# An edge mask and edge counts built in DRAM tables by indirect DMAs, in place of one-hot matrix products

## What is computed

```python
def _build_mask(edge_index, edge_type, edge_type_weights, dtype):
    src, dst = (edge_index[0], edge_index[1])
    w = jax.nn.softplus(edge_type_weights)
    mask = jnp.full((N, N), -jnp.inf, dtype=dtype)
    mask = mask.at[src, dst].set(w[edge_type - 1])        # the last edge wins
    diag = jnp.diagonal(mask)
    mask = mask.at[idx, idx].set(jnp.where(jnp.isneginf(diag), w[3], diag))
...
scores = jnp.einsum('hnd,hmd->hnm', q2, k2) * scale + mask[None]   # layer 0, 16 heads
...
deg = jax.ops.segment_sum(jnp.ones_like(col), col, num_segments=n) # layer 1, 4 hops
dis = jnp.clip(deg, 1.0) ** (-0.5)
norm = dis[row] * dis[col]
msg = norm[:, None] * alpha * x_j                                  # one per edge
agg = jax.ops.segment_sum(msg, col, num_segments=n)
```

## Time and profile before

| | us |
|---|---|
| median of 3 runs | 799.48 (799.28 to 799.86) |
| the profiled execution, its own time | 800.38 |
| its span in the profile | 798.6 |
| PE busy in the span | 775.6 (97%) |
| DVE busy | 583.9 (73%) |
| ACT busy | 387.0 (48%) |
| POOL busy | 48.2 (6%) |

### The profile page before, as it was taken

The page is one execution under the profiler, slowest core; times in us unless marked ns, Lnnn a source line. Parts: engine busy times, 40 slices in busy tenths (PEclk is TensorE's granted clock), DMA queues, the critical chain, the costliest instruction groups (busy, mean ns, idle before and its releaser), DMA issues. The chain is left out here.

```text
span 798.6 us, 11507 instructions
## 1 busy us (share of the span) xinstructions
PE 775.6 (97%) x4270; PEld 685.8 (86%) x4270; DVE 583.9 (73%) x1234; ACT 387.0 (48%) x800; POOL 48.2 (6%) x88
## 2 busy tenths in 40 slices
PE   5999999999999999999998899999999999999998
PEld 5888878889999999998875488888888879999886
DVE  7988888646644798997688968889886676674341
ACT  5222113344533676765767646574683342454220
POOL 3000000000000000001102211000002020000000
PEclk9999999999999999999999999999999999999999
DMA  5522114433334333319975349224134245334331
GB/s 190 185 81 78 56 56 138 137 118 106 106 125 129 103 100 97 95 55 319 269 244 129 132 121 261 96 89 158 53 124 128 72 113 138 133 133 158 126 125 39
DMA packets 28775, 102.17 MB, mean 128 GB/s; under 512 B 3736, under 2 KB 3864, under 8 KB 28464
## 3 DMA queue, kind: packets, MB, share of 16 engines
q1 hardware_dynamic: 24784, 86.76, 32.3%
q0 software_dynamic: 3936, 14.68, 8.4%
HBM read 91.99 MB, written 1.57 MB: 117 GB/s over the span
## 5 line engine op out<-in xcount | busy, mean ns | idle before, releaser
L1200 DVE TENSOR_TENSOR w_lo<-raw,w_hi 128x1024 fp32r<-128x1024 f32 x140 | 169.9, 1222 | 65.1 <-ACT w_hi L910 64.7
L910 ACT ACTIVATE w_hi<-raw 128x1024 fp32r<-128x1024 f32 x140 | 147.3, 1057 | 105.7 <-PE bank L1984 79.6
L1932 PE MATMUL bank<-xn1T,w_hi 128*128 128x384 f32 x416 | 106.8, 337 | 0.0
L1984 PE MATMUL bank<-w_hi,xn3T 128*128 128x512 f32 x288 | 92.0, 393 | 0.0
L1932 PEld LDWEIGHTS bank<-xn1T,w_hi 128*128 128x128 f32 x416 | 74.2, 188 | 0.9 <-issue 0.3
L1932 PE MATMUL bank<-xn1T,w_lo 128*128 128x384 f32 x208 | 69.6, 335 | 0.0
L1984 PEld LDWEIGHTS bank<-w_hi,xn3T 128*128 128x128 f32 x288 | 54.1, 188 | 11.0
L1932 PE MATMUL bank<-xn4T,w_hi 128*128 128x384 f32 x240 | 61.1, 335 | 0.0
L1984 PE MATMUL bank<-w_lo,xn3T 128*128 128x512 f32 x144 | 56.0, 389 | 0.0
L1932 PEld LDWEIGHTS bank<-xn4T,w_hi 128*128 128x128 f32 x240 | 43.2, 188 | 0.0
L1932 PE MATMUL bank<-xn4T,w_lo 128*128 128x384 f32 x120 | 40.1, 335 | 0.0
(11 more groups left out here) (363 smaller groups left out, 1712.0 us busy)
## 6 DMA issues: line engine op xcount, KB each, us to landing
raw<-weights SPq DMA_DIRECT2D x140, 512.0 KB, 3.3
row_sb<-rows SPq DMA_DIRECT2D x6, 512.0 KB, 5.6
kcat<-kcat POOLq DMA_DIRECT2D x16, 192.0 KB, 2.9
base<-rows POOLq DMA_DIRECT2D x6, 512.0 KB, 13.8
w2r<-w_in SPq DMA_DIRECT2D x1, 2048.0 KB, 10.5
w1r<-w_in POOLq DMA_DIRECT2D x1, 2048.0 KB, 9.7
x_sb<-x_in SPq DMA_DIRECT2D x3, 512.0 KB, 4.9
row_sb<-rows SPq DMA_DIRECT2D x6, 256.0 KB, 4.8
```

The source lines that it names most:

```text
L910: act.activation(w_hi[:, u % RING], raw[:, u % RAW], ACT.Copy).then_inc(hi_split, 1)
L1200: dve.tensor_tensor(w_lo[:, u % RING], raw[:, u % RAW], f(w_hi[:, u % RING]), ALU.subtract).then_inc(unit_split, 1)
L1932: last = pe.matmul(out_of(pr)[:, 0:N], w[pa][:, slot, k * P:(k + 1) * P], TT[src][:, pb, k], start=(k == 0 and m == 0), stop=(k == KD - 1 ...
L1984: last = pe.matmul(out_of(pr)[:], tile[:, pa, k, ts], w[pb][:, at_, j * HALF:(j + 1) * HALF], start=(kk == 0 and j == 0 and m == 0 and nam ...
```

## The change

The mask and the counts are built in two tables in DRAM, each of 384x384 numbers and 512 spare cells. POOL fills them with zeros or with the value for no edge, by two plain DMAs, and then writes the edges by indirect DMAs, one for each chunk of 128 edges and table, four chunks to a step: 48 that write the value of the edge's type to the mask table, 48 that add to the count table, and three that write the diagonal first. Since one edge may hit the cell of another, each step of 512 edges is freed of duplicates before: DVE now compares each chunk with all four chunks of its group (L1331 after the change, 128x512), with a triangular matrix `later` that gives 4096 for a later edge and 1 otherwise. The sum of a row is 4096 or more where a later edge of the step has the same cell, and such an edge is sent to a spare cell; else it is the number of edges of the step in that cell, which is what is added to the count. A step's four writes to a table wait until the four of the step before have landed. At the end POOL loads both tables back into SBUF. The one-hot products and matrices, and the steps graph, counts and mask, are gone. The products for degrees and norms move from the v2 units to behind k1.5 and k1.6. The units v1 and mk now take the banks 0, 1 and 2 in turn, and the keys alternate between the banks 7 and 6.

The diff, cut to its core:

```diff
-    for i in range(GROUPS):
-        run("v1", i, i + 1) if i < KD else run("mk", i - KD, i - KD + 1)
-        if i:
-            steps.append(("graph", i - 1))
-        if i < GROUPS - 1:
-            steps.append(("edges", i))
...
+    q = 0
+    for n in range(KD + 4 + 8):
+        run("v1", n, n + 1) if n < KD else run("mk", n - KD, n - KD + 1) if n < KD + 4 else run("v2", n - KD - 4, n - KD - 3)
+        if q < GROUPS and n == 3 * q // 2:
+            steps.append(("edges", q))
+            q += 1
...
-    run("k1", 1, 8)
+    run("k1", 1, 6)
+    steps.append(("degree",))
+    run("k1", 6, 7)
+    steps.append(("norm",))
+    run("k1", 7, 8)
...
+            def scatter(tab, n, src, **how):
+                return pool.indirect_dma_start(tab[:, :], bass.IndirectOffsetOnAxis(ap=place[:, n:n + 1].bitcast(U32), axis=0),
+                                               src, None, **how)
...
+            link(pool.memset(mask[:], 8 * NO_EDGE))
+            pool.dma_start(tiles_of(mask_table), mask[:]).then_inc(mask_clear, 16)
...
+            link(pool.memset(count[:], 0.0))
+            pool.dma_start(tiles_of(count_table), count[:]).then_inc(count_clear, 16)
             for s in STEPS:
+                if s == ("edges", 0):
+                    pool.wait_ge(mask_clear, 16)
+                    pool.wait_ge(w8_ready, 1)
+                    pool.wait_ge(consts, 7)
+                    for t in range(NT):
+                        scatter(mask_table, EC + t, w8[:, 2, NTYPE - 1:NTYPE]).then_inc(scattered, 16)
+                    pool.wait_ge(count_clear, 16)
+                    pool.wait_ge(valued, 1)
+                    for q in range(GROUPS):
+                        pool.wait_ge(placed, q + 1)
+                        pool.wait_ge(scattered, 16 * (NT + 4 * q))
+                        for c in range(4 * q, 4 * q + 4):
+                            scatter(mask_table, c, value[:, c:c + 1]).then_inc(scattered, 16)
+                        if q:
+                            pool.wait_ge(summed, 16 * 4 * q)
+                        for c in range(4 * q, 4 * q + 4):
+                            scatter(count_table, c, total[:, c:c + 1], compute_op=ALU.add).then_inc(summed, 16)
+                    pool.wait_ge(scattered, 16 * (NT + EC))
+                    pool.dma_start(mask[:], tiles_of(mask_table)).then_inc(mask_ready, 16)
+                    pool.wait_ge(summed, 16 * EC)
+                    pool.dma_start(count[:], tiles_of(count_table)).then_inc(counted, 16)
...
-                    ins = dve.scalar_tensor_tensor(same[:, c % 2], out_of(pr)[:, j * P:(j + 1) * P], key[:, c:c + 1],
-                                                   later[:], ALU.is_equal, ALU.mult, accum_out=dead[:, c:c + 1])
+                    ins = dve.scalar_tensor_tensor(same[:, c % 2], out_of(pr)[:], key[:, c:c + 1],
+                                                   later[:, (3 - j) * P:(7 - j) * P], ALU.is_equal, ALU.mult,
+                                                   accum_out=total[:, c:c + 1])
...
+                link(dve.scalar_tensor_tensor(spare[:, sl], total[:, sl], LATER, beyond[:], ALU.is_ge, ALU.mult))
+                dve.tensor_tensor(place[:, sl], spare[:, sl], flat[:, sl], ALU.max).then_inc(placed, 1)
...
+                if kind == "edges":
+                    for q in (0, 1) if s[1] == 0 else (s[1] + 1,) if s[1] + 1 < GROUPS else ():
+                        keys(q)
...
-                    pe.wait_ge(counted, NT)
+                    pe.wait_ge(counted, 16)
```

More of the change, by code:

```diff
@@ L33 @@
 NO_EDGE = -1.0e30
[L34 removed]
+LATER = 4096.0
 GROUPS = EC // 4
@@ L92, in schedule @@
     steps.append(("transpose", "xn1"))
-    for i in range(GROUPS):
-        run("v1", i, i + 1) if i < KD else run("mk", i - KD, i - KD + 1)
-        if i:
-            steps.append(("graph", i - 1))
-        if i < GROUPS - 1:
-            steps.append(("edges", i))
-        if i == GROUPS - 2:
-            steps.append(("edges", GROUPS - 1))
-    steps.append(("graph", GROUPS - 1))
-    steps.append(("counts",))
-    run("v2", 0, 3)
-    steps.append(("degree",))
-    run("v2", 3, 4)
-    steps.append(("norm",))
-    for k in range(NTYPE):
-        run("v2", 4 + k, 5 + k)
-        steps.append(("mask", k))
+    q = 0
[4 more added lines that the diff above has]
+            q += 1
     run("mv", 0, 4)
@@ L313, in plan_banks @@
                 if name in ("v1", "mk"):
-                    product(f"{name}.{i}", 0 if (name, i) == ("v1", 0) else 6, u)
+                    product(f"{name}.{i}", i % 3, u)
                 elif name in ("q2", "k2"):
@@ L328, in plan_banks @@
                     group += 1
-        elif kind == "graph":
-            if s[1] + 1 < GROUPS - 1:
-                product(f"keys.{s[1] + 1}", 7)
-            if s[1] == GROUPS - 3:
-                product(f"keys.{GROUPS - 1}", 7)
-            if s[1] == GROUPS - 1:
-                for t in range(NT):
-                    product(f"last_edge.{t}", t)
-                    product(f"count.{t}", 3 + t)
+        elif kind == "edges":
+            for q in (0, 1) if s[1] == 0 else (s[1] + 1,) if s[1] + 1 < GROUPS else ():
+                product(f"keys.{q}", 7 - q % 2)
         elif kind == "transpose":
-            if s[1] == "xn1":
-                product("keys.0", 7)
             for k in range(KD):
@@ L576, in gps_kernel, with table, tiles_of @@
         power_in = at("power_in", [P, NT], F32, SMALL + 3)
+        place = at("place", [P, EC + NT], I32, SMALL + 3.75)
+        value = at("value", [P, EC], F32, SMALL + 4)
+        total = at("total", [P, EC], F32, SMALL + 4.25)
+        def table(name):
+            return nc.dram_tensor(name, (N * N + 4 * P, 1), F32, kind="Internal").ap()
+        def tiles_of(tab):
+            return tab[0:N * N].rearrange("(t p m) o -> p t (m o)", p=P, m=N)
+        mask_table, count_table = table("mask_table"), table("count_table")
         bank = [ctx.enter_context(nc.psum_tensor(f"bank{b}", [P, 512], F32)) for b in range(8)]
@@ new lines, in _ @@
+            link(pool.memset(later[:], LATER))
+            pool.affine_select(out=later[:], in_=later[:], compare_op=ALU.is_gt, fill=1.0, base=-3 * P,
+                               pattern=[[1, 7 * P]], channel_multiplier=-1).then_inc(consts, 1)
+            link(pool.iota(beyond_i[:], pattern=[[P, 4]], base=N * N, channel_multiplier=1))
+            pool.tensor_copy(beyond[:], beyond_i[:]).then_inc(consts, 1)
+            for t in range(NT):
+                ins = pool.iota(place[:, EC + t:EC + t + 1], pattern=[[1, 1]], base=t * P * (N + 1), channel_multiplier=N + 1)
+                if t:
+                    ins.then_inc(consts, 1)
@@ L1366, in _ @@
                 if kind == "edges":
-                    edge_group(s[1])
-                if kind == "graph":
                     if s[1] == 0:
@@ L1380, in _ @@
                         dve.tensor_scalar(w8[:, 2], w8[:, 2], 8.0, None, ALU.mult).then_inc(w8_ready, 1)
-                if s == ("graph", GROUPS - 1):
-                    for t in range(NT):
-                        pr = f"last_edge.{t}"
-                        wait_full(dve, pr)
-                        dve.tensor_scalar(no_edge[:, t], out_of(pr)[:, 0:N], 0.0, 8 * NO_EDGE, ALU.is_equal, ALU.mult)
-                        emptied(dve.tensor_scalar(edge_cls[:, t], out_of(pr)[:, 0:N].bitcast(I32), 23, 3,
-                                                  ALU.logical_shift_right, ALU.bitwise_and), pr)
+                        dve.wait_ge(w8_ready, 1)
+                        link(dve.tensor_scalar(value[:], cls[:], 0.0, w8[:, 2, 0:1], ALU.is_equal, ALU.mult))
+                        for k in range(1, NTYPE):
+                            link(dve.tensor_scalar(chosen[:], cls[:], float(k), w8[:, 2, k:k + 1], ALU.is_equal, ALU.mult))
+                            ins = dve.tensor_tensor(value[:], value[:], chosen[:], ALU.add)
+                            if k == NTYPE - 1:
+                                ins.then_inc(valued, 1)
+                            else:
+                                link(ins)
                 if kind == "transpose":
```

130 lines of the change are left out of this document (24 added, 106 removed).

## The result

| | before | changed | later: degrees moved too | later, and mk in other banks |
|---|---|---|---|---|
| median us | 799.4 | 779.1 | 771.1 | 766.0 |
| range us | 799.1 to 799.9 | 772.0 to 784.2 | 770.2 to 772.7 | 765.3 to 768.7 |
| ratio to before, 95% | 1 | 0.9715 (0.9687 to 0.9742) | 0.9645 (0.9633 to 0.9658) | 0.9587 (0.9574 to 0.9600) |

The change makes the kernel 20.3 us faster in the median. The forecast was 770.4, with a range of 763 to 788. So the sign and the range held, but the median is 8.7 us above the forecast, and executions of the changed kernel are up to 12 us apart, where those of before lie within 2 us, but for one at 802.6.

What follows compares the result with a forecast made beforehand. PE, busy 97% of the span, was taken as the bound. 36.5 us at most, less 7.9 of waits and 0.4 of keys, with rounding of the walk, gave 29.1: 799.5 - 29.1 = 770.4 us, range 763 to 788.

Steps and rivals of the forecast that it cites:

- What PE loses: Twelve graph steps of 2.95 us leave PE; with diagonal products and 0.6 us of idle, some 36.5 us at most.
- What comes in on DVE: Wide comparisons cost DVE 3.6 us a group; 12.7 us against PE's 13.4 for three units, so DVE just keeps up.
- The walk: Stepping through PE's and DVE's order with earlier durations: PE waits 7.9 us in all, v2.0 starts at 77.0.
- v2, degrees and norms: v2 stretch: 2.9 us of degrees and norms leave, 1.3 of keys enter; mv 32.0 us earlier, net gain 29.1.
- What comes in on POOL: POOL's chain of 96 indirect DMAs ends at 166 us, 44 us before the degrees behind k1.5 need the count table.
- price s: POOL time for one indirect DMA, taken as 1.2 us; PE waits from 1.66, all gain gone at 1.96.
- The other limit, landing: On POOL, a group lasts 4s plus landing if longer than 8s: 7.2 to 13.6 us against 13.3 available.
- tables in time: Forecast's own case: no PE wait on a DMA before the degrees; 770.4 us, 763 to 778, chance 0.74.
- late by less than the gain: Rival: PE waits 2 to 26 us for the tables before the degrees, taken as 15; 785 us, chance 0.07.
- DVE too slow: Rival: wide comparisons cost 0.25 us more each, all 12 groups push PE, 12 us lost; 782 us, chance 0.06.
- the loads as a bound: Rival: weight loads, not PE, bound the shortened units; no time of its own, no separate chance.
- the tiny writes as 273 ns each: Rival: POOL's groups take 17.5 us, PE waits 51 us for the tables; 821 us; slower has chance 0.10.

Runs made afterwards that it cites:

- later: degrees moved too: Changed kernel with degrees moved from behind k1.5 to behind k2.0 and norms from behind k1.6 to behind q2.0: 771.1 us, ratio 0.9645.
- later, and mk in other banks: Changed kernel with degrees behind k2.0, norms behind q2.0, and the mk units in banks 3 to 5 instead of 0 to 2: 766.0 us, ratio 0.9587.
- first profile: Profile of the changed kernel's fastest execution of the first four: 772.0 us, 770.2 in the span.
- second profile: Changed kernel run again with no edit, median 779.0 us; the profile caught an execution of 778.6 us, with PE waiting 5.5 us for the count load.
- the banks alone: Changed kernel with only the mk units moved to banks 3 to 5, degrees and norms left behind k1.5 and k1.6: 779.6 us.

## Why the prediction was right, and where it was not

**What PE loses** held. The pace of keys and units is that of the earlier trace rows; PE is busy 33.7 us less.

**What comes in on DVE** held in size: the wide comparison took 739/751/753 ns (smallest, median, largest), where the earlier trace rows gave 750, and comparisons stand 0.79 us apart. The walk overstated the waits: keys.2 1.2 for 1.7, keys.4 0.6 for 1.6, keys.8 nothing for 1.0, v2.0 2.9 for 3.6; 4.7 us for 7.9. v2.0 began at 74.6, not 77.0. (The 22.5 us at which the walk has DVE finish "the low part of v1.0" is the end of another row, the addition of the bias; nothing hangs on the name.) The bank clash at v2.0, found in the order alone, is the largest of them, and an edit of one number takes it away.

**v2, degrees and norms**: mv began at 111.9, against about 111. That these agree within 1 us is luck, two errors that cancel: 3.2 us less waiting, of which 2.4 were left at v2.0, and 2.6 us of the lower clock behind the ekT wait, a term that the sum lacked. It had read a clock of 1.00 off and kept it for a stretch with new idle time. The closing sum does not add up by itself either: 36.5 - 7.9 - 0.4 is 28.2, and the 0.9 up to 29.1 stand there as rounding of the walk; 29.1 follows from the walk alone.

**What comes in on POOL** is the step that failed, in its price s. From below 0.52 us was right as a bound, and no row bounded it from above; 1.2 was "the nearest row plus a third". Measured, a writing scatter takes 0.96, an adding one 1.56, and each has 0.30 us behind it: (0.96 + 1.56) / 2 + 0.30 = 1.56 alone, and 1.67 to 1.76 in eight profiles, with the time lost beside DVE (below), a term that s had at nothing. The formula was right: with s = 1.67 it gives an end at 51 + 160 = 211, where the table landed at 209.7. The threshold of 1.66 us was right within 0.03: that execution, at 1.67, had 1.9 us left, and the profile with the 5.5 us wait has 1.73. The other limit, landing, never bound: in the two profiles of the changed kernel POOL idled for it at most 0.3 us in all 12 groups together.

So the forecast's own case, tables in time, is three of ten executions of the changed kernel (771.7 to 772.0), and the median is the rival "late by less than the gain" (the other seven, from 777 up), which had 0.07 of the chance. That the first profile showed tables in time was luck, and that the median still lies inside the range is due to the range, which took in that rival. It gave 15 us of waiting for 785; the 5.5 us and the clock behind them of the second profile were nearer. DVE too slow, the loads as a bound, and the tiny writes as 273 ns each did not occur. The estimate of 803 us by the Trainium skill's fixed cost of 2.0 us in line (DMA: Bandwidth & Descriptors, Anatomy of one DMA) did not come about either: the chain of 96 took 160 us and not 192, and POOL's next DMA began 0.30 us behind the last while landing took 3.6.

## What to carry to other kernels

A chain that is moved to an idle engine has a deadline; work out the slack for the highest price that no row excludes, and if it can vanish, move the step that needs the chain to a later place where its bank is free, which here gave 8 us. When a gain on the bounding engine does not show in the time, look for the next step that waits for another engine: the banks alone gave 0, with the deadline moved 5.1. And look at a kernel's spread: executions 10 us apart, where those of before agreed within 2, were for the most part a race between two chains, and one profile showed only its lucky side.

## What the runs showed of the hardware

**POOL's scatters lose time when they begin inside DVE's subtraction.** Eight profiles have the same scatters in the same order. In each of them the adding scatters that begin while a w_lo instruction of DVE runs, 13 to 18 of the 48, took 1.85 to 2.08 us in the mean, up to 2.67; the others took 1.57 to 1.60. Writing scatters took 1.46 to 1.64 there and 0.97 to 1.01 elsewhere. Of the scatters that begin with more than 0.2 us of a w_lo ahead of them, 86 of 89 adding ones end 1.42 to 1.48 us behind the end of that w_lo and 96 of 97 writing ones 0.83 to 0.87, which is their usual duration less 0.1: they stand still until it is over. The 46 adding scatters that begin inside a comparison of DVE took 1.56 us, like those beside an idle DVE. The timeline of POOL and then of DVE in the changed kernel, second profile:

```profile
201.33 1.56 POOL L795 DMA_INDIRECT count_table<-total,place  x1 [0.30 <-issue]
203.19 1.94 POOL L795 DMA_INDIRECT count_table<-total,place  x1 [0.30 <-issue]
205.44 1.55 POOL L795 DMA_INDIRECT count_table<-total,place  x1 [0.30 <-issue]
```
```profile
201.54 0.62 DVE L1210 SCALAR_TENSOR_TENSOR k1T<-bank,bias,k1T 128x384 fp32r<-128x384 f32 x1 [1.99 <-ACT k1T L918]
202.49 1.23 DVE L1217 TENSOR_TENSOR w_lo<-raw,w_hi 128x1024 fp32r<-128x1024 f32 x1 [0.33 <-ACT w_hi L927]
```

The scatter that begins at 203.19, inside the w_lo of 202.49 to 203.72, takes 0.39 us more than its neighbours. The one before it, which was under way when that w_lo began, takes 1.56.

How often and how early in a w_lo the scatters begin differs between executions, and that moves the end of the chain. In the eight profiles 22 to 31 of the 96 scatters begin inside a w_lo and take 8.5 us (the first profile of the changed kernel) to 16.6 us more than 0.96 or 1.55 each. The 96 last 160.4 to 168.9 us, and without that time 151.4 to 152.6 in all eight. The count load went out between 203.3 and 213.8 us. The Trainium skill, GPSIMD Engine Reference (Specifications), says that this engine's way to SBUF is shared with VectorE and contended by DVE instructions with two SBUF inputs; w_lo has two (raw, w_hi), and the trace agrees. No run took the w_lo instructions away from the scatters, so this rests on the times of these profiles.

**The clock behind a wait.** After the same wait of 2.8 to 3.0 us for ekT, products ran at the half level for some 5 us in three of eight profiles (granted clock 0.69 from 71 to 82 us), for part of that time in two, and not at all in three. Behind the four waits of 5.5 to 40 us in front of the degrees these took 4.00 us in place of 2.06 each time, and 3.97 and 3.98 behind the two waits of 3.6 us for oT.

**Writing scatters can stop the other engines.** At one each 1.27 us, DVE stood for 40 us with its input ready, ACT stood too, SP waited for DVE, and PE started a product each 0.3 to 3.5 us, until POOL paused; DVE moved again 1.4 us behind the end of the last scatter. From 75.6 us on the starts of PE's products lie 0.7 us or a multiple of it apart. With adding scatters between them, or with one of the count scatters in flight at a time, nothing stopped. The Trainium skill, DMA: Bandwidth & Descriptors (Queues, rings and completion order), has each DMA engine take turns between its queues; that is not contradicted: SP's queue moved nothing for 35 us (68 to 103), but had nothing to move, while POOL's had 1.8% of the engines' time. So the DMA engines were not what was short. What is held, whether it is the release of a waiting engine, the fetch of instructions or something else, stays open.
